# A tile kept during the second sweep is fetched as one 1 MB transfer every fourth unit instead of two 512 KB halves, one every second unit

## The reference

```python
hx = implicit_filter(z, Xw..)          # 256 x 64, from a small network
hy = implicit_filter(z, Yw..)
k  = outer product of hx and hy, per channel
out = irfft2(rfft2(x) * rfft2(k))[..., :256, :256] + x * bias
# whitening
x1  = out as (64 channels, all pixels)
x1_s = x1[:, ::9]
mean = mean(x1_s);  cov = x1_s @ x1_s.T / n + 0.01 * I
deconv = inverse square root of cov, 5 Newton-Schulz steps
result = deconv @ (x1 - mean)
```

## Time and profile before

| | |
|---|---|
| time, median of 3 executions | 921.83 us (921.45 to 923.97) |
| the profiled execution: own time | 924.23 us |
| the profiled execution: span | 922.4 us |
| busy share PE, VectorE, ScalarE, GpSimd | 94%, 62%, 55%, 54% |
| data moved by DMA | 294.08 MB, 319 GB/s on average |

### The profile page before, as it was taken

One profiled execution on the slowest core, in us unless ns is written; L12 is line 12 of the kernel. 1 busy time (PEld: TensorE's weight loads), 2 busy tenths in 40 slices (PEclk: granted clock), 3 DMA queues, 4 the chain that ended last, 5 costly groups with the idle time before them and its releaser, 6 DMA issues.

```text
span 922.4 us, 16409 instructions
## 1 busy us (share of the span) xinstructions
PE 869.4 (94%) x6252; PEld 730.4 (79%) x6252; DVE 574.2 (62%) x630; ACT 511.2 (55%) x974; POOL 494.1 (54%) x279
## 2 busy tenths in 40 slices
PE   7999999999999999999999999998999999877773
PEld 5999999999999999999999999998544444323221
DVE  3488888788888867878778877875333333322221
ACT  2677777777777757777667767661133333222120
POOL 1498888888888866878778877873000000000000
PEclk9899999999999999999999999999999999999997
DMA  3798888888888886999999999988999999999998
GB/s 124 243 291 278 265 263 261 262 264 259 268 254 267 265 240 219 326 315 313 303 327 318 322 320 317 307 284 276 411 398 428 427 427 426 427 428 426 427 427 350
DMA packets 82948, 294.08 MB, mean 319 GB/s; under 512 B 13301, under 2 KB 31926, under 8 KB 68278
## 3 DMA queue, kind: packets, MB, share of 16 engines
q1 hardware_dynamic: 82785, 292.91, 89.7%
q10 hardware_dynamic: 85, 0.12, 0.0%
HBM read 155.37 MB, written 137.61 MB: 318 GB/s over the span
## 4 chain that ended last, share of the span: by engine, by line
PE 80%; DMA 13%; DVE 1%; SPq 1%; ACT 1%; issue 1%; POOL 0%; DVEq 0%; ACTq 0%; POOLq 0%
PE ps L735 23%; PE ps L854 16%; PE ps L732 13%; PE ps L733 13%; PE ps L734 13%; DMA arena<-convolved 11%; PE ps L774 2%; DMA filters<-arena 1%; PE ps L709 1%; DMA arena<-filters 1%; DMA first_filters<-arena 1%; PE ps L794 0%; SPq L290 0%; ACT arena L526 0%; SPq L329 0%
## 5 line engine op out<-in xcount | busy, mean ns | idle before, releaser
L735 PE MATMUL ps<-arena 128*128 128x128 f32 x2048 | 394.1, 274 | 0.0
L732 PE MATMUL ps<-rounded 128*128 128x256 f32 x1024 | 373.9, 365 | 5.4 <-DVE rounded L606 3.1
L429 POOL TENSOR_TENSOR arena<-arena,mask 128x1024 f32<-128x1024 f32 x126 | 326.0, 2587 | 68.5 <-DVE arena L594 68.1
L735 PEld LDWEIGHTS ps<-arena 128*128 128x128 f32 x2048 | 317.3, 191 | 0.0
L734 PE MATMUL ps<-rounded 128*128 128x256 f32 x1024 | 289.7, 283 | 0.0
L733 PE MATMUL ps<-rounded 128*128 128x256 f32 x1024 | 288.5, 282 | 0.0
L854 PE MATMUL ps<-arena 128*128 128x512 f32 x488 | 216.0, 597 | 27.6 <-DMA arena<-convolved 27.6
L594 DVE SCALAR_TENSOR_TENSOR arena<-arena,bias_sb,ps 128x1024 f32<-128x1024 f32 x127 | 162.5, 1280 | 89.8 <-DMA convolved<-arena 45.6
L854 PEld LDWEIGHTS ps<-arena 128*128 128x128 f32 x488 | 90.7, 190 | 151.9 <-issue 105.0
L732 PEld LDWEIGHTS ps<-rounded 128*128 128x128 f32 x1024 | 196.6, 192 | 6.9 <-issue 5.1
L394 POOL TENSOR_TENSOR rounded<-arena,rounded 128x512 fp32r<-128x512 f32 x128 | 164.8, 1287 | 67.2 <-ACT rounded L473 66.9
(11 more groups left out here) (100 smaller groups left out, 296.8 us busy)
## 6 DMA issues: line engine op xcount, KB each, us to landing
arena<-x SPq DMA_DIRECT2D x128, 512.0 KB, 5.1
convolved<-arena SPq DMA_DIRECT2D x256, 256.0 KB, 4.7
out<-arena SPq DMA_DIRECT2D x64, 1024.0 KB, 14.1
arena<-convolved SPq DMA_DIRECT2D x47, 1024.0 KB, 19.1
arena<-filters SPq DMA_DIRECT2D x246, 80.0 KB, 4.0
arena<-convolved SPq DMA_DIRECT2D x28, 512.0 KB, 5.2
filters<-arena SPq DMA_DIRECT2D x4, 768.0 KB, 6.2
rounded<-convolved SPq DMA_DIRECT2D x3, 1024.0 KB, 10.4
```

Of the source, the lines that this page charges most:

```text
L429: nc.gpsimd.tensor_tensor(masked_of(k, 0, PER), by_image(y_sb[k]), mask_of(q // C, 0, PER), ALU.mult).then_inc(masked_done, 1)
L732: mm(wide, hi[:, b, cols], t_hi[k][:, f, :], start=True, stop=False)
L735: last = mm(o[:, b, m * S + P:(m + 1) * S], block1[:, b, cols], t_f32[k][:, f, :], start=False, stop=True)
```

## The change

One half of a kept tile every second unit becomes a whole tile every fourth unit, in the same place of SP's queue. The number of bytes, their source and their destination are the same: 14 tiles of 1 MB. The last piece before is issued in iteration q = 122, the last tile of the change in q = 120. Each partition gets one run of 8 KB where it got two of 4 KB.

```diff
-PIECES = 2
 ...
             def load_kept(q):
-                n = (q - (C + 4)) // 2
-                if q % 2 or not 0 <= n < KEPT * PIECES:
-                    return
-                w = TW // PIECES
-                lo = n % PIECES * w
+                t = (q - (C + 4)) // 4
+                if q % 4 or not 0 <= t < KEPT:
+                    return
 
                 for k in range(2):
                     sp.wait_ge(y_stored[k], 32 * (C // 2))
-                sp.dma_start(kept[:, n * w:(n + 1) * w], tile_in(n // PIECES, lo, lo + w)).then_inc(kept_loaded, 16)
+                sp.dma_start(kept[:, t * TW:(t + 1) * TW], tile_in(t, 0, TW)).then_inc(kept_loaded, 16)
 ...
                 if t < KEPT:
-                    pe.wait_ge(kept_loaded, 16 * KEPT * PIECES)
+                    pe.wait_ge(kept_loaded, 16 * KEPT)
```

## The result

The change made the kernel slower: 930.0 us (927.61 to 934.86, 10 runs) against 923.06 us for the kernel before, a ratio of 1.0085 with a 95% interval of 1.007 to 1.0101. One of the ten executions before took 2985.37 us and is not in the ratio; the two medians lie 6.9 us apart, 0.75%. The forecast was no change, 922.0 us with a range of 920.2 to 926.0. The profiled execution took 932.69 us, its span is 930.9 us; before they were 924.23 and 922.4.

A forecast was written before the change was run, and what follows sets the result against it. TensorE (PE) was taken to bound both sweeps, DMA the last stage. 924.23 - 0.72 + 0.9 idle gave 924.4 us for the profiled execution; from the median, 921.83 + 0.2 = 922.0 us, range 920.2 to 926.0.

The forecast's parts named there:

- The step on the longer block: DMA queues, second sweep: x and y stores behind a whole tile come 1.23 us later (1.66 at the sweep's rate).
- Does it reach PE?: Second sweep, late y stores: PE loses 0.1 us at the worst place, nothing at a typical one; total idle 0.9 us.
- the forecast's typical case: Store behind a kept piece in the second sweep: 6.9 + 1.23 - 7.1 = 1.0 us late, costing PE nothing.
- the distance of four units: Between blocks in the second sweep: VectorE can work off 3.8 us of lateness, against 1.9 us in two units.
- The rival "slower": Second sweep: five places without slack each pass 1.23 us to PE, 6.2 us in all, 928.0 us; chance 0.13.
- the forecast's margin of 0.1 us: Slowest store in the second sweep: VectorE 2.5 us late at a slack of 2.38, so PE loses 0.1 us.
- The fixed cost of about 2 us: Each DMA transfer: 14 fewer would take 28 us off DMA work, which no row can turn into time.
- ring order: One DMA queue's descriptors are consumed in order, so x and stores behind a tile wait for the whole of it.

The follow-up runs named there:

- f1_three_y: The changed kernel with three y buffers instead of two and 13 kept tiles instead of 14; ratio 0.9996 to the kernel before.
- experiment 4: The changed kernel with its 1 MB tiles issued ahead of the filter pieces, ratio 0.9998 to the kernel before, or from ScalarE's queue, 1.0052.
- h1_stores_first: The changed kernel with the two stores of y issued ahead of the same iteration's x load; ratio 1.0252 to the kernel before.
- h3_two_tiles: The changed kernel with two 1 MB tiles back to back every eighth unit, seven times; ratio 1.0179 to the kernel before.
- f2_kept13: The changed kernel with 13 kept tiles instead of 14 and still two y buffers; ratio 1.0096 to the kernel before.

## Why the prediction was wrong

**What held.** PE bounds the sweep and the loss could only come as PE idle time; the first sweep and the last stage kept their length; the 14 issues take the same time on SP (0.53 us each); the packets of 8 KB or more rise by 1792, from 14670 to 16462, as a run of 8 KB that goes as one packet should make them; VectorE waits fewer times for stores, and SP waits at more of its x loads (18, where it was 8). The step on the longer block was sized well: the slower store directly behind a tile lands after 8.2 us on average over the 14 places, and before after 6.9 at the same ones, so 1.3 us more against the 1.23 to 1.66 forecast, and 9.9 us at the longest for 9.6. VectorE also gets back into rhythm at about the forecast pace: after the stop at 485.69 the slack of the filter split grows from 0.10 to 1.08, 1.91 and 2.38 us in the next three units.

**What failed** is the step "Does it reach PE?", in its tolerance: "a store that lands within 7.1 us costs VectorE nothing". It took the 2.2 us from L594 to the second store's issue from the undisturbed rhythm of the first sweep. At the 14 places behind a tile it is 2.4 to 4.0 us, 3.3 on average (2.9 at the same places before). So a typical store is 3.3 + 8.2 - 9.28 = 2.2 us late where the prediction had 1.0, and that alone nearly uses up the slack of 2.38. At the place shown above L591 starts at 471.07 and the second store is issued at 474.42, so 3.35 us, because SP has the filter pieces, the tile and x in front of it while VectorE, catching up from the stop before, delivers this y only 3.66 us after the one before it, at a rhythm of 4.64. So 9.28 - 3.35 = 5.9 us is the tolerance there, and the store took 9.3: VectorE is 3.4 us late at a slack of 2.38, which gives 1.0 us for PE; it is 1.2 to 1.4 in the trace. The trace of before had this already: the second store of the pair at 565.24 is issued at 565.76, and its L594 starts 2.96 us earlier:

```profile
562.80 1.28 DVE L594 SCALAR_TENSOR_TENSOR arena<-arena,bias_sb,ps 128x1024 f32<-128x1024 f32 x1 [0.65 <-DMA convolved<-arena]
```

I compared the landing with a rhythm that the place does not have. Part of the difference seems to be the stops' own doing. In `f1_three_y`, where VectorE never waits for a store and SP has the same tile in front of the stores, the numbers are 2.6 + 7.7 - 9.28 = 1.0 us late, the forecast's typical case; with two buffers a late VectorE makes the next y closer to the one before, and SP falls behind it. The landing has its part as well: behind the tile of 377.34 VectorE was in rhythm and the second store was issued after 2.55 us, but it took 9.0 us to land. How much is SP's lateness and how much the scatter of the landing is read from the timeline; no experiment isolates it.

**The forecast relied on the distance of four units** to bring the slack back before the next block. It does come back, and it does not help: even from full slack a single tile passes it. At 385.17 us the slack of PE is 2.38; one unit later, behind the tile issued at 377.34, it is 0.10. So the loss comes behind ten of the 14 tiles, 0.1 to 1.4 us each by the length of the unit and 2.8 at the last.

**The rival "slower"** had its size nearly right (6.2 us, where the stops cost 7.3) and its place right, the stores behind a tile. Its reason, lateness that adds up from block to block at five places, was not what happened. I gave it 0.13 because I tested the forecast's margin of 0.1 us (2.5 us late at a slack of 2.38) only at its middle. A margin that small, at 14 places, should have made the two cases about even. The clock, a further 1.5 us in the profiled execution, was in no case.

**The Trainium skill.** The Trainium skill's rule for the most bandwidth, 1 MiB or more per transfer (DMA: Bandwidth & Descriptors, Rules for kernel authors), did not pay here: the DMA share did fall, from 0.96 to 0.91, and the kernel got slower. The fixed cost of about 2 us that the prediction took from this page of the Trainium skill is a fit for transfers issued by GpSimd (section Anatomy of one DMA), and here SP issues them; the share of 0.91 over 271.1 us against 0.96 over 265.0 is some 8 us of busy time less, not 28. What the Trainium skill says on ring order (same page, Queues, rings and completion order) told the direction, and experiment 4 agrees for the stores, which land after 6.9 us instead of 8.2 once the tile has a queue of its own. It is not the whole story: from that queue the tile still costs 0.52%.

## What to carry to other kernels

A fetch that nobody waits for still has a place in a queue, and what stands behind it may be needed soon: judge its size by the slack of the next transfers in line, not by the efficiency of the transfer. Measure that slack in the very iteration where the block stands, from the instruction that makes the data to the landing and with the queue engine's lateness in it, not in the undisturbed rhythm. And look at what was the last to finish before a stop, not only at the name that the profile gives: in the changed kernel it gave none, in `h1_stores_first` GpSimd, and both times the filter split of VectorE had ended 0.10 us before. If slack is short, move the block in front of something that has room before changing its size: the order ahead of the filter pieces took away all PE idle time with halves, and brought the 1 MB tiles from 1.0085 back to 0.9998.

## What the runs showed of the hardware

An idle stretch of 2.59 us on PE, after dense work, was followed by 3.4 us at half the granted clock, and the stops of 1.2 us and less in the same sweep were not. In `h3_two_tiles` stops of 2.37 and 1.81 us were followed by such a stretch too, but one of 2.27 us in the same kernel was not, nor was one of 2.64 us in `h1_stores_first` or one of 2.57 us in `f2_kept13`. So the length of a stop alone did not decide it here: the drop is a risk, not a fixed price. Transfers over 64 partitions kept the DMA engines at a share of 1.00 where the same bytes over 128 partitions took 0.95, at nearly the same rate (308 and 309 GB/s).
